# Two transformer layers with mixtures of experts on one core: order words read later, row numbers copied ahead, layer 1's tiles sorted by levels, attention's first step reordered

## The reference, cut to what matters

```
# layer 0: attention of 16 heads from the side input onto x, with a mask by length, then 24 experts, top 2
q, k, v = projections;  w = softmax([q k_prev^T, q k_self]);  a = (w v) Wo + bo
topk_val, topk_idx = top_k(a gate_w + gate_b, 2);  combine = softmax(topk_val)
x = x + a + sum_k combine_k * (gelu(a w1[e] + b1[e]) w2[e] + b2[e])
# layer 1: masked pooling with learned scores, then 8 experts, top 2, and a shared expert
scores = tanh(x W1 + b1) v;  p = softmax(mask(scores));  h = (p x) / count
topk_w, topk_i = top_k(softmax(h gate_w^T), 2), normed and times 2.5
x = x + sum_k topk_w_k * (silu(h wg[e]) * (h wu[e])) wd[e] + shared(h)
```

## Time and profile before

| | us |
|---|---|
| median of three runs | 437.19 (435.76 to 439.93) |
| the profiled execution, its own time | 436.51 |
| its span, first to last instruction | 434.7 |
| attention and its last stages | up to about 176 |
| first product of layer 0's experts | 181.36 |
| last send of layer 0's results | 278.25 |
| first tile of layer 1 | 350.76 |
| last send of layer 1's results has landed | 420.78 |
| TensorE busy | 372.5 (86% of the span) |
| VectorE, ScalarE, GpSimd busy | 281.0, 247.2, 198.7 |

### The profile page before, as it was taken

The page is one execution under the profiler, slowest core; times in us unless marked ns, Lnnn a source line. Parts: engine busy times, 40 slices in busy tenths (PEclk is TensorE's granted clock), DMA queues, the critical chain, the costliest instruction groups (busy, mean ns, idle before and its releaser), DMA issues.

```text
span 434.7 us, 10203 instructions
## 1 busy us (share of the span) xinstructions
PE 372.5 (86%) x2635; PEld 268.8 (62%) x2635; DVE 281.0 (65%) x1114; ACT 247.2 (57%) x742; POOL 198.7 (46%) x270
## 2 busy tenths in 40 slices
PE   3699999999999995399999899559988879999920
PEld 2356656666666653299999899226556547777710
DVE  3766787887887888366666466369575626666615
ACT  1288888788888783255665456237975114444400
POOL 3551143444433444634454555422747606666630
PEclk9999999999999997599999999759999989999975
DMA  7400999987777703366766676050111122323217
GB/s 153 76 15 13 315 355 228 242 185 165 176 193 188 141 15 98 93 171 177 200 172 182 176 191 193 17 185 15 50 37 44 56 51 78 90 76 82 68 46 248
DMA packets 61072, 57.14 MB, mean 131 GB/s; under 512 B 6042, under 2 KB 49703, under 8 KB 60768
## 3 DMA queue, kind: packets, MB, share of 16 engines
q1 hardware_dynamic: 56288, 48.10, 44.4%
q0 software_dynamic: 4736, 8.47, 5.8%
HBM read 36.12 MB, written 21.73 MB: 133 GB/s over the span
## 4 chain that ended last, share of the span: by engine, by line
PE 70%; DVE 7%; DMA 7%; issue 4%; ACT 3%; POOL 3%; SPq 2%; DVEq 1%; POOLq 0%; ACTq 0%
PE bank L735 13%; PE bank L863 8%; PE bank L1062 7%; PE bank L868 7%; PE bank L744 6%; PE bank L758 5%; PE bank L1079 2%; PE bank L1070 2%; PE bank L1080 2%; DMA w<-in_L_ffn_w_dram 2%; POOL layer_rows L703 2%; DMA qexp<-layer_outputs 2%; PE bank L788 2%; PE bank L774 1%; PE bank L838 1%
## 5 line engine op out<-in xcount | busy, mean ns | idle before, releaser
L1107 ACT ACTIVATE ps<-bank,ntop 128x128 f32<-128x128 f32 x256 | 73.6, 379 | 12.9 <-DVE ntop L1367 12.9
L1174 ACT ACTIVATE hT<-bank,w 128x128 f32<-128x128 f32 x176 | 51.0, 369 | 43.8 <-PE bank L863 43.4
L735 PE MATMUL bank<-qexp 128*128 128x512 f32 x128 | 67.7, 611 | 3.2 <-POOL qexp L645 2.7
L715 POOL DMA_INDIRECT layer_outputs<-w_all x40 | 38.9, 972 | 34.1 <-issue 20.4
L744 PEld LDWEIGHTS bank<-ident,ps 128*128 128x128 f32 x256 | 31.9, 141 | 33.3 <-issue 29.6
L863 PE MATMUL bank<-xT,w 128*128 128x128 f32 x352 | 49.3, 285 | 2.7 <-DMA w<-in_L_ffn_w_dram 1.2
L642 POOL TENSOR_TENSOR qexp<-kA,rowmask 128x512 f32<-128x512 f32 x16 | 16.6, 1039 | 73.2 <-DVE kA L1451 73.2
L1116 ACT ACTIVATE pT<-bank 128x512 f32<-128x512 f32 x64 | 38.6, 603 | 19.7 <-PE bank L744 18.4
L1366 DVE TENSOR_REDUCE mx<-bank 128x4 f32<-128x512 f32 x64 | 43.7, 683 | 7.5 <-PE bank L735 6.2
L863 PEld LDWEIGHTS bank<-xT,w 128*128 128x128 f32 x352 | 44.4, 198 | 4.7 <-issue 3.9
L703 POOL DMA_INDIRECT layer_rows<-rows_all,places x32 | 30.9, 966 | 23.8 <-DVE rows_all L1733 9.4
(11 more groups left out here) (312 smaller groups left out, 811.2 us busy)
## 6 DMA issues: line engine op xcount, KB each, us to landing
w<-in_L_ffn_w_dram SPq DMA_DIRECT2D x44, 258.0 KB, 3.4
layer_rows<-fill SPq DMA_DIRECT2D x10, 910.0 KB, 9.1
w_all<-in_L_ffn_w_dram SPq DMA_DIRECT2D x24, 256.0 KB, 5.1
qexp<-layer_outputs SPq DMA_DIRECT2D x8, 512.0 KB, 4.8
xt<-layer_rows SPq DMA_DIRECT2D x45, 65.0 KB, 2.5
w_all<-layer_rows SPq DMA_DIRECT2D x40, 65.0 KB, 1.8
xfT<-in_xfT_dram SPq DMA_DIRECT2D x16, 128.0 KB, 2.8
layer_rows<-fill SPq DMA_DIRECT2D x1, 1560.0 KB, 11.3
```

The lines of the kernel that those rows point to most:

```text
L715: g.indirect_dma_start(ys1_dram, bass.IndirectOffsetOnAxis(ap=xt1[r][:, P:P + 1].bitcast(U32), axis=0), yb1[r][:, :], None, bounds_check=Y ...
L735: pe.matmul(psA[g % 2][:, :], qexp[b % 2][:, g, :], kexp[b % 2].rearrange("p g k -> p (g k)"), start=True, stop=True).then_inc(a_in_ps, 1)
L1107: m = s.activation(ps[g % 2][:, t, :], psA[g % 2][:, t * P:(t + 1) * P], ACT.Exp, bias=ntop[:, h:h + 1])
L1174: s.activation(hT[r % 2][:, c, :], banks[c][:, 0:P], ACT.Gelu, bias=w1[r][:, F0 + c:F0 + c + 1]).then_inc(gelu_done, 1)
```

## The change

- **Start of attention.** ScalarE runs one exponential on the identity matrix first. VectorE makes `lens`, `haslen`, `keymask`, `rowmask`, `valid` for two sequences and `headmask` before it waits for the bias products. `kexp` of sequence 0 is made by VectorE after `prod` instead of by GpSimd. `valid` is made for two sequences at the end of each of steps 1 to 7, and `types_constants` runs at the end of step 8.
- **Order words.** TensorE reads three words in the last step of attention, in front of a wait, and the other three in the tiles 12, 16 and 20; VectorE reads one in each fourth tile.
- **Extra tiles.** GpSimd copies the row numbers of tile j+1 after it has sent tile j, and waits for the slot's earlier send first.
- **Layer 1.** Tiles are sorted by level: the first tile of each expert, then the second of each, and so on. The table is made on 128 partitions (`order_tiles`, two parts), turned by TensorE (`turn_table`, ahead of `shared_down(2)`), and packed by a shorter `plan1` after shared(3,0); places are packed three to a word. `bound_blocks` finds after how many tiles each of the blocks 0 to 2 is complete. SP loads these blocks as soon as so many tiles' results have landed (in its list after the loads of all tiles), and only the last block after all. Results are added in place, without `ob`. There are 8 slots instead of 10.
- Waits on `pnT` and `pl_in_ps` are added, and three more constants.

```diff
-RING1 = 10
+RING1 = 8
@@ sync @@
             for j in range(TILES1):
                 r, n = j % RING1, j // RING1
+                if j % 3 == 0:
+                    word = sp.value_load(place1[0:1, j // 3:j // 3 + 1], min_val=0, max_val=256 ** 3 - 1)
                 if n > 0:
                     sp.wait_ge(y1_sent[r], 16 * n)
-                m = sp.value_load(place1[0:1, j:j + 1], min_val=0, max_val=XS_TILES - 1)
+                m = clamped((word // 256 ** (j % 3)) % 256, XS_TILES - 1)
                 sp.dma_start(xt1[r][:, :], xs1_j[bass.ds(m, 1)]...).then_inc(xt1_in[r], 16)
+            sp.wait_ge(bounds1_ready, 1)
+            for k in range(NB - 1):
+                bound = sp.value_load(bounds1[0:1, k:k + 1], min_val=BLK * 2, max_val=TILES1)
+                for r in range(RING1):
+                    sp.wait_ge(y1_sent[r], (bound + (RING1 - 1 - r)) // RING1 * 16)
+                load_results(k)
             for r in range(RING1):
                 sp.wait_ge(y1_sent[r], 16 * (TILES1 // RING1))
-            for k in range(NB):
-                sp.dma_start(yy[k], ys1_t[:, BLK * k:BLK * (k + 1), :, :]).then_inc(yy_in[k], 16)
+            load_results(NB - 1)
@@ gpsimd, expand @@
+                if b > 0:
+                    pool.wait_ge(kA_ready, b + 1)
+                    g.tensor_tensor(kexp[b % 2], ...)
@@ gpsimd, extra tiles @@
+            g.tensor_copy(row_r[0][:, :], idx[:, E0:E0 + 1]).then_inc(copied, 1)
             with pool.Fori(0, nr) as n:
                 for r in ring:
                     j = RING * n + r
                     pool.wait_ge(y_ready, E0 + 1 + j)
-                    g.tensor_copy(row_r[r][:, :], idx[:, bass.ds(j + E0, 1)]).then_inc(copied, 1)
                     pool.wait_ge(copied, j + 1)
                     carry(pool)
                     send_results(row_r[r][:, 0:1], r)
+                    q = (r + 1) % RING
+                    pool.wait_ge(y_out[q], 16 * (E0 // RING + n + (r + 1) // RING))
+                    g.tensor_copy(row_r[q][:, :], idx[:, bass.ds(j + E0 + 1, 1)]).then_inc(copied, 1)
@@ tensor @@
+                if i == STEPS - 1:
+                    pe.wait_ge(order_ready, 1)
+                    words0.extend(order_word(pe, n) for n in range(3))
                 if active(i, 6):
...
-            pe.wait_ge(order_ready, 1)
-            words0 = [order_word(pe, n) for n in range(E0 // RING)]
...
+                if j % RING == 0 and j // RING >= 3:
+                    words0.append(order_word(pe, j // RING))
@@ scalar @@
+            act.wait_ge(pool_const, 2)
+            s.activation(gelu_warm[:, :], ident[:, 0:1], ACT.Exp)
@@ vector @@
+                if i == 1:
+                    dve.wait_ge(rows_masked, 1)
+                    dve.wait_ge(kA_ready, 1)
+                    v.tensor_tensor(kexp[0], ...).then_inc(kexp_ready, 1)
...
+                if 2 * i < B:
+                    valid_keys(2 * i)
+                    cc.join()
+                if 2 * i == B:
+                    types_constants()
...
-            words0 = [order_word(dve, n) for n in range(E0 // RING)]
+            words0 = []
...
+                if j % RING == 0:
+                    words0.append(order_word(dve, j // RING))
...
             shared(2, 1)
+            order_tiles(0)
             shared(2, 2)
+            order_tiles(1)
+            shared(3, 0)
             plan1()
-            shared(3, 0)
...
+                if j == RING1:
+                    bound_blocks()
...
-                v.tensor_tensor(ob[k % 2][:, :, :], yy[k][:, :, 0, :], x2[:, blk, :], ALU.add).then_inc(ob_ready, 1)
+                v.tensor_tensor(yy[k][:, :, 0, :], yy[k][:, :, 0, :], x2[:, blk, :], ALU.add).then_inc(ob_ready, 1)
+            def order_tiles(part):
+                levels, tiles = iota_k[:, 1:LEVELS1 + 1], ntf1[:, NB - 1, :]
+                if part == 0:
+                    ... nti1, ntf1: tiles of each expert after each block
+                    cx.link(v.tensor_tensor(under_level[:, :, :], levels..., tiles..., ALU.min))
+                    cx.link(v.tensor_reduce(at_level[:, :], under_level[:, :, :], AX_X, ALU.add))
+                    ... past1, under1
+                if part == 1:
+                    ... nine small operations to table1, on the partition of each tile
```

More of the change, by code:

```diff
@@ L43 @@
 TILES1 = B * P * 2 // P + E1
-RING1 = 10
+RING1 = 8
+LEVELS1 = 2 * B // 2
+WORDS1 = (TILES1 + 2) // 3
 FILL_TILES = 14
@@ L242, in attention_moe_kernel @@
         gs1 = sb("gs1", [P, BLK, 2])
-        nti1 = sb("nti1", [1, E1], I32)
-        ntf1, incl1 = sb("ntf1", [1, E1]), sb("incl1", [1, E1])
+        nti1 = sb("nti1", [P, NB, E1], I32)
+        ntf1 = sb("ntf1", [P, NB, E1])
+        under_level = sb("under_level", [P, LEVELS1, E1])
+        at_level, past1, under1 = (sb(n, [P, LEVELS1]) for n in ("at_level", "past1", "under1"))
+        lev1, base1, turn1 = (sb(n, [P, 1]) for n in ("lev1", "base1", "turn1"))
+        alive1, prefix1, sel1 = (sb(n, [P, E1]) for n in ("alive1", "prefix1", "sel1"))
+        table1 = sb("table1", [P, 2])
+        most1 = sb("most1", [P, NB - 1])
+        upto1 = sb("upto1", [P, NB - 1, E1])
+        bound1 = sb("bound1", [P, NB - 1])
+        bounds1 = sb("bounds1", [P, NB - 1], I32)
         spare = aux[:, B * P:(B + E0) * P]
-        past1, beneath1 = (spare[0:1, TILES1 * E1 * i:TILES1 * E1 * (i + 1)].rearrange("p (j e) -> p j e", e=E1) for i in range(2))
-        ej1, tj1 = sb("ej1", [1, TILES1]), sb("tj1", [1, TILES1])
-        expert1 = sb("expert1", [1, TILES1])
         words1 = sb("words1", [1, TILES1 // 8], I32)
-        place1 = sb("place1", [1, TILES1], I32)
+        place1 = sb("place1", [1, WORDS1], I32)
         pow8 = sb("pow8", [1, 8])
-        scaled1 = sb("scaled1", [1, TILES1])
+        pow256 = sb("pow256", [1, 3])
+        scaled1 = sb("scaled1", [1, 3 * WORDS1])
+        wordp1 = sb("wordp1", [1, WORDS1])
         wordf1 = sb("wordf1", [1, TILES1 // 8])
@@ L386, in attention_moe_kernel @@
         ob_ready = sem("ob_ready")
-        ob_out = [sem(f"ob_out{i}") for i in range(2)]
+        ob_out = sem("ob_out")
+        table1_ready = sem("table1_ready")
+        table1_in_ps = sem("table1_in_ps")
+        bounds1_ready = sem("bounds1_ready")
         psT = banks[0:2]
@@ L990, in shared_down, with turn_table @@
                 y.then_inc(out_acc, 1)
+            def turn_table():
+                pe.wait_ge(table1_ready, 1)
+                for n in range(2):
+                    m = pe.transpose(ps_chain[0][0:1, n * P:(n + 1) * P], table1[:, n:n + 1], ident[:, :])
+                m.then_inc(table1_in_ps, 1)
             pe.wait_ge(y_ready, E0 + nr * RING)
@@ L1037, in _ @@
             shared(3, 0)
+            turn_table()
             shared_down(2)
@@ L1320, in _, with valid_keys @@
             dve.wait_ge(w_att, 16 * 2)
+            cc.link(v.tensor_copy(lens[:, :], lens_i))
+            cc.add(v.tensor_scalar(haslen[:, :], lens[:, :], 1.0, -1.0, ALU.is_ge, ALU.mult))
+            cc.add(v.tensor_scalar(keymask[:, :], lens[:, :], iota_p[:, 0:1], None, ALU.is_gt))
+            assert cc.k == KEYS_MASKED
+            cc.link(v.tensor_reduce(rowmask[:, :], ind[:, :].rearrange("p (g j) -> p g j", g=NG), AX_X, ALU.add))
+            v.tensor_scalar(rowmask[:, :], rowmask[:, :], 0.0, None, ALU.is_gt).then_inc(rows_masked, 1)
+            def valid_keys(b):
+                cc.add(v.tensor_tensor(valid[:, b:b + 2, :], iota_k[:, :].unsqueeze(1).broadcast_to([P, 2, P]),
+                                       lens[:, b:b + 2].unsqueeze(2).broadcast_to([P, 2, P]), ALU.is_lt))
+            valid_keys(0)
+            cc.add(v.tensor_reduce(headmask[:, :], ind[:, :].rearrange("p (g j) -> p j g", g=NG), AX_X, ALU.add))
+            assert cc.k == HEADS_MASKED
             dve.wait_ge(cb_in_ps, 1)
@@ new lines, in plan1 @@
+            def plan1():
+                dve.wait_ge(table1_in_ps, 1)
+                experts, places = ps_chain[0][0:1, 0:TILES1], ps_chain[0][0:1, P:P + 3 * WORDS1]
+                cx.link(v.tensor_tensor(scaled1[:, :].rearrange("p (w t) -> p w t", t=3), places.rearrange("p (w t) -> p w t", t=3),
+                                        pow256[:, :].unsqueeze(1).broadcast_to([1, WORDS1, 3]), ALU.mult))
+                cx.link(v.tensor_reduce(wordp1[:, :], scaled1[:, :].rearrange("p (w t) -> p w t", t=3), AX_X, ALU.add))
+                cx.add(v.tensor_copy(place1[:, :], wordp1[:, :]))
+                cx.link(v.tensor_tensor(scaled1[:, 0:TILES1].rearrange("p (w t) -> p w t", t=8), experts.rearrange("p (w t) -> p w t", t=8),
```

96 lines of the change are left out of this document (49 added, 47 removed).

## The result

The changed kernel takes 428.6 us in the median of six runs (427.3 to 431.5), the kernel before 436.9 beside it (five of its six runs lie between 435.4 and 439.9, one took 1256.7). So the changed kernel is faster by 1.7%; the medians are 8.3 us apart, where 12.3 were forecast. The profiled execution took 431.0 (span 429.2, 5.5 us less than the 434.7 before).

What follows compares the result with a forecast made beforehand. TensorE was taken to bound attention and expert tiles, with other links at the start, before the first tiles, in the routing's end and the tail. Terms summed to -12.3 us, giving a median of 424.9; range 420.5 to 430.5.

Steps and rivals of the forecast that it cites:

- start: Start of attention: scores can start at 10.3 instead of 14.88, minus 4.6 us (bounds minus 3.5 to minus 5.0).
- moved to the attention steps: Attention steps 1 to 8: VectorE's moved small operations mostly fit its free 1.77 us a step; plus 0.5, at most 5.1.
- order words, first product: Between attention and expert tiles: TensorE reads three words earlier, first product at 178.45 instead of 181.36, minus 2.9.
- words inside the loop, to tile 3: Layer 0's tiles: order words read inside the loop by TensorE and VectorE cost plus 0.3, upper bound 2.0 for TensorE's.
- extra tiles, to the last send: End of layer 0: GpSimd's period stays, only the first send after a gap comes sooner; minus 0.4, bounds 0 and minus 1.0.
- routing: Layer 1's routing: the table delays shared_down(2) and later work, plus 1.5; taken as plus 0.8 because TensorE's clock may stay up.
- tail: After the last landing: one load, two additions, one store, 7.7 to 7.9 us where 13.85 stood; minus 6.1.
- A step longer than 9.36: Sign of being wrong: an attention step taking more than the 9.36 us that TensorE was busy in one step.
- The recorded signs: Layer 0: first product about 7.5 us earlier than 181.4, last send about 7.6 us earlier.
- the ring: Layer 1's tiles: 8 slots starve above 12.2 us round trip, put at 11.0; chances 0.03 to 432.8, 0.03 to 441.6, 0.02 more.
- the forecast's own case: Whole kernel: all four gains arrive, 421 to 428 us; chance 0.62.
- the clock case: Layer 1's routing: a new 2 us gap before shared_down(2) drops TensorE to 1.2 GHz; plus 3, 428 us; chance 0.13.

Runs made afterwards that it cites:

- e3: The changed kernel with TensorE and VectorE reading all six order words before tile 0 again; 456.2 us on a slower chip.
- e7: The changed kernel with type constants made in step 2, VectorE's order word one position later, table turned behind shared_down(2); ratio 0.9735 to the kernel before, slower chip.
- e4: The changed kernel with the row numbers copied in their own tile again, after y_ready; 455.2 us on a slower chip.

## Why the prediction was right, and where it was not

Point by point, in us of the profiled executions, forecast and measured:

```
start                                  -4.6   -4.9
moved to the attention steps           +0.5   +1.25
order words, first product             -2.9   -3.05
words inside the loop, to tile 3        +0.3   +0.9
extra tiles, to the last send          -0.4   -0.65
mixing to layer 1's first products      0     +0.8
routing                                +0.8   +1.5
tile loop (first to last transpose)    +0.1   +3.6
last transpose to last landing          0     +0.7
tail                                   -6.1   -5.7
sum                                   -12.3   -5.5
```

- **Start**: right, steps and size: 4.5 of the 4.6 by the steps forecast, and 0.4 more from the earlier landing of an input, which no step foresaw. Whether the two engines get in each other's way was hardly tried, as the times forecast had qexp and kexp[0] one behind the other: qexp (1.04 us) and kexp[0] overlap by 0.11 us. The earlier trace rows say more than the stretch that was read from them: `valid` ended at 13.94 and qexp, begun at 12.0, 0.9 us after it, in about the time it takes alone. It looks stopped while `valid` ran, not slowed.
- **Moved operations**: the mechanism right, the size low. The overflow of VectorE in step 8 was put at 0.4 and stopped ScalarE and TensorE for 1.2. A step longer than 9.36 was a recorded sign of being wrong, and this one came.
- **Order words**: right (e3 puts back about 3). The 0.9 up to the third tile is no cost of VectorE's word, as e3 and e7 expected, but TensorE's clock coming up later, a term that the forecast did not have; from the third tile on TensorE is 5.7 to 5.9 us ahead of before for twenty tiles, so its own reads inside the loop (tiles 12, 16 and 20) cost nothing that shows.
- **Extra tiles**: the 0.65 is not the row numbers' gain. It is what TensorE gained in this stretch (1.3 us) less what GpSimd fell behind (0.7), and e4 can't tell the copy's share from none. The recorded signs put the first product 7.5 and the last send 7.6 us earlier, where the forecast's own terms give 7.0 and 7.1; it came to 6.7 and 6.5.
- **Routing**: the step was right, +1.5 before the clock. I took off 0.7 for a clock that would stay up: it did stay up at the loop's start (three first products at 0.85 us, where the earlier trace rows has 1.44), which saved 1.4 us of the loop, as before its third and fourth transposes came 0.65 and 0.73 late. But the loop then lost it at 370. The 0.8 lost ahead of the routing is clock too: eight products of L979 took 2.00 us at 285.22, in the chain before 1.17.
- **Last landing**: of the 0.7, 0.5 is GpSimd, whose sends behind the last tiles took 1.43, 1.02 and 1.23 us where they took 0.97, and 0.2 the landing itself (2.36, not 2.14).
- **Tail**: right within 0.4; the one load left took 4.0, not 3.6.
- **The step that failed** is the ring, which I kept out of the sum as a rival with chances of 0.03, 0.03 and 0.02. The margin was named correctly, 12.2 less 11.0 being 1.2 us (measured 1.1), but for another loop: a place's whole round trip, where the loop that binds is the one of R-3 tiles. For 8 places both give nearly the same margin; for 5 mine gave 86 us and the chip 131. (That 11.0 came so close is partly luck: its 7.0 from transpose to send is the last tile's, whose result waits 2.6 us for GpSimd, and the others take 6.6.) And the landing stood in it as a constant of 2.14, from one row, though the spread of that line in the trace before reaches 4.4. A margin of 1.2 against a spread of 2.2 is not a rival at 0.08, it is a term of the sum, which had it at nothing: +5.0 with the clock loss in the profiled execution. The recorded sign for it, TensorE waiting for tile rows in layer 1's loop, came, with 1.94 us. How much of it the median has no trace shows; as the median is 2.4 us shorter than the profiled execution, about 3 us is an estimate. The median missed the forecast of 424.9 by 3.7.

The median of 428.6 is inside the range of 420.5 to 430.5, but above the 421 to 428 of the forecast's own case, and on the profiled execution's 431.0 the range would have failed. It held because three of the four gains, on which the sum rests, came to within 0.5 us of their forecasts (the fourth, 0.4 for the row numbers, is not shown), and because the loss, named and left out of the sum, is no larger in the median than the clock case that the range was stretched for. The second is luck.

## What to carry to other kernels

A ring's margin is its places less the depth of the software pipeline, times the tile's period, less one turn of the loop that the order of instructions closes; set it against the largest landing of the line, not the median. Before a gain is counted at a stage's start, ask who closes the stage: TensorE finished layer 0's products 7.2 us earlier, GpSimd, at 2.04 us a send, only 6.5. When an operation has become longer, look at its clock before looking for a wait. And when all small work of one kind is moved into one step, it comes as one block and its price is that of the engine waiting behind it.

## What was not expected of the hardware

- On three of four chips in the experiments all kernels lose 21 to 29 us to stalls of 2 to 10 us, with the same instructions stopped in each kernel (ScalarE's L1264 for 7.4 to 9.6 us, VectorE's rank addition for 2 to 5), all in straight-line code of layer 1's routing, and to a slower tile loop, in which GpSimd's sends go out 1.35 us behind their results, not 0.77, at about every third tile. The releaser is none that the profile shows; the cause is open.
- The same products of tile 0 with w2 (L901), behind the same work, ran at granted clocks of 0.51 to 1.00 in the changed kernels, from 1.92 down to 1.06 us. What decides is open.
- Indirect sends of one line land in 2.2 to 4.3 us, loads of 65 KB in 1.8 to 3.7, within one execution.
